# Tile loop of a fused decoder kernel: a tile's outputs and the next tile's transposes in one section behind all projections of a step, the transposes in the gates' banks

## What is computed

```python
gate, hBC, dt = x @ in_proj_w.T, split              # 8192 gate, 8192 + 2*8*128 conv channels, 128 dt
hBC = silu(causal_conv4(hBC) + conv_b)              # 4 taps along the tokens
hs, Bm, Cm = split(hBC)
L = exp(segsum(dt * -exp(A_log)))                   # decay from token to token, per head
y = (Cm @ Bm.T * L) @ (hs * dt) + hs * D            # per head, 128 x 128 tokens
g = y * silu(gate)
g = g * rsqrt(mean over a group's 1024 channels of g*g + eps) * norm_w
x = layernorm(x + g @ out_proj_w.T)
```

## Time and profile before

| | |
|---|---|
| median of the runs shown | 1745.28 us |
| the profiled execution: its own time | 1743.17 us |
| its span, first to last instruction | 1741.5 us |
| TensorE matmul busy | 1659.1 us (95%) |
| VectorE busy | 1196.1 us (69%) |
| ScalarE busy | 1103.3 us (63%) |
| GpSimd busy | 710.6 us (41%) |
| ACT_TABLE_LOADs at L531 / L512 / L546 | 64 / 71 / 8, mean 1283 ns |
| mean granted TensorE clock | 0.988 |

### The profile page before, as it was taken

One profiled execution on the slowest core, in us unless ns is written; L12 is line 12 of the kernel. 1 busy time (PEld: TensorE's weight loads), 2 busy tenths in 40 slices (PEclk: granted clock), 3 DMA queues, 4 the chain that ended last, 5 costly groups with the idle time before them and its releaser, 6 DMA issues.

```text
span 1741.5 us, 26304 instructions
## 1 busy us (share of the span) xinstructions
PE 1659.1 (95%) x9160; PEld 1275.5 (73%) x9160; DVE 1196.1 (69%) x2257; ACT 1103.3 (63%) x2352; POOL 710.6 (41%) x588
## 2 busy tenths in 40 slices
PE   6899999999999999999999999999999987889998
PEld 4777787778777877787778777877787765444656
DVE  4775758675867586758685868586858676896443
ACT  3675668575847594759474948494849482996231
POOL 3363536352626263626361636164616352331000
PEclk8999999999999999999999999999999988999999
DMA  5232213221323131313131313131413273001000
GB/s 200 70 113 73 97 63 120 73 97 55 122 78 98 49 121 64 118 43 128 55 127 43 127 54 128 43 122 48 140 34 115 65 104 111 1 1 37 13 13 24
DMA packets 76551, 138.88 MB, mean 80 GB/s; under 512 B 6786, under 2 KB 13954, under 8 KB 76164
## 3 DMA queue, kind: packets, MB, share of 16 engines
q1 hardware_dynamic: 76420, 137.21, 24.9%
HBM read 134.55 MB, written 2.63 MB: 79 GB/s over the span
## 4 chain that ended last, share of the span: by engine, by line
PE 44%; DVE 33%; ACT 15%; issue 6%; DMA 1%; SPq 1%; POOL 0%; DVEq 0%; ACTq 0%
DVE conv L729 13%; PE ps_hs L1093 6%; PE ps_hs L1095 6%; PE ps_hs L1094 6%; ACT ps_dec L531 6%; DVE xdt L753 4%; DVE m_sb L762 4%; ACT L531 3%; ACT sq_tmp L541 3%; PE ps_hs L246 3%; PE ps_y L1320 3%; PE ps_hs L1282 3%; PE ps_dec L1282 3%; PE ps_hs L248 3%; PE ps_hs L247 3%
## 5 line engine op out<-in xcount | busy, mean ns | idle before, releaser
L378 POOL TENSOR_SCALAR_AFFINE_SELECT cum_bc<-cum_bc 128x1024 f32<-128x1024 f32 x128 | 141.4, 1105 | 501.5 <-DMA cum_bc<-cum_scratch 501.5
L729 DVE SCALAR_TENSOR_TENSOR conv<-ps_hs,cw,conv 128x508 f32<-128x508 f32 (+2 forms) x432 | 319.6, 740 | 36.8 <-ACT conv L495 26.6
L531 ACT ACTIVATE ps_dec<-cum_bc,neg_cum 128x128 f32<-128x128 f32 x1024 | 308.8, 357 | 0.8
L762 DVE TENSOR_TENSOR m_sb<-ps_dec,cb 128x512 f32<-128x512 f32 x256 | 169.6, 686 | 154.6 <-ACT ps_dec L531 154.6
L246 PE MATMUL ps_hs<-x_hi,w_hi 128*128 128x512 f32 x576 | 231.9, 403 | 15.6 <-DVE conv L729 7.6
L246 PE MATMUL ps_gate<-x_hi,w_hi 128*128 128x512 f32 x576 | 239.5, 416 | 0.0
L495 ACT ACTIVATE conv<-ps_hs,cbias,cw 128x512 f32<-128x512 f32 x144 | 110.6, 769 | 189.5 <-PE ps_hs L248 189.5
L248 PE MATMUL ps_gate<-x_hi,w_lo 128*128 128x512 f32 x576 | 226.3, 393 | 0.0
L1093 PE MATMUL ps_hs<-wo_hi,g_hi 128*128 128x512 f32 x512 | 204.4, 399 | 22.8 <-DVE acc L889 8.4
L247 PE MATMUL ps_hs<-x_lo,w_hi 128*128 128x512 f32 x576 | 225.6, 392 | 0.0
L248 PE MATMUL ps_hs<-x_hi,w_lo 128*128 128x512 f32 x576 | 225.6, 392 | 0.0
(11 more groups left out here) (141 smaller groups left out, 3092.8 us busy)
## 6 DMA issues: line engine op xcount, KB each, us to landing
cum_bc<-cum_scratch SPq DMA_DIRECT2D x128, 512.0 KB, 4.0
w_raw<-w_in SPq DMA_DIRECT2D x145, 256.0 KB, 4.6
wo_raw<-w_out SPq DMA_DIRECT2D x64, 256.0 KB, 4.9
g_acc<-x_t SPq DMA_DIRECT2D x4, 512.0 KB, 6.8
acc<-x_nat SPq DMA_DIRECT2D x1, 2048.0 KB, 9.4
k_rep<-ctx_t SPq DMA_DIRECT2D x8, 256.0 KB, 12.6
out<-y_out SPq DMA_DIRECT2D x8, 256.0 KB, 2.0
wg_sb<-w_gate SPq DMA_DIRECT2D x1, 1792.0 KB, 12.4
```

Source lines behind the costliest of these rows:

```text
L531: x = sc.activation(ps_dec[e][:, cols], cum_bc[bh][:, e, cols], ACT.Exp, bias=neg_cum[:, bh * HB + b, head:head + 1])
L729: v.scalar_tensor_tensor(out=dst, in0=src, scalar=cw[:, at, TAPS - 1 - n:TAPS - n], in1=dst, op0=ALU.mult, op1=ALU.add).then_inc(S["tap"], 1)
L762: v.tensor_tensor(flat(m_sb[:, q]), ps_dec[q % 2][:, :], flat(half(cb, q // 2)), ALU.mult)\
```

## The change

Every engine's order in the tile loop is rewritten. TensorE issues heads and gates of step s+1, both halves each, then (each fourth tile) the out-products of the tile before, then outputs(t, 0), outputs(t, 1) and the eight transposes of step s+1, now into ps_gate; they wait for both gates of that tile to have been read (sg_ok), and the next step's gates wait for scale_dt (xdt_ok). Combine, squares and g_low of a tile move into the step behind it on VectorE, ScalarE and GpSimd. ScalarE's order in a tile step becomes: decay 0, squares half 0 of the tile before, first_tap, squares half 1, decay 1, first_tap, silu, decay 2, gate, silu, decay 3, gate, scale_out. The sums of out-products (`keep_products`) stand behind decay 3 on VectorE. outputs(t, 0) also wait for both g_low of the tile before. In a step of B and C the out-products, square_sums and cb_products stand behind the projections. The diff, cut:

```diff
@@ -401,10 +401,14 @@
                 if s + 2 < STEPS:
...
                 if holds_bc(s):
+                    if s:
+                        add_square(tile_at(s - 1), 0)
+                        add_square(tile_at(s - 1), 1)
                     continue
...
                 j = t % TPH
-                if j:
+                if t % TPG:
+                    add_square(t - 1, 0)
                     add_square(t - 1, 1)
@@ -416,9 +420,8 @@
                 pool.wait_ge(S["wo_hi_ok"], t + 1)
...
                                  ALU.subtract).then_inc(S["wo_lo_ok"], 1)
-                add_square(t, 0)
-                if j == TPH - 1:
-                    add_square(t, 1)
+            add_square(TILES - 1, 0)
+            add_square(TILES - 1, 1)
             pool.wait_ge(S["gate_ps"], 2 * STEPS)
@@ -524,6 +527,8 @@
                     act.wait_ge(S["neg_cum_ok"], bh + 1)
...
                     act.wait_ge(S["bc_ok"], 2 * t + bh + 1)
+                if t % TPG == 0 and bh == 0:
+                    act.wait_ge(S["cb_sb"], 2 * (t // TPG) + e + 1)
                 need(act, S["m_ok"], 4 * t + q - 1)
@@ -550,51 +555,61 @@
                     first_tap(0, sub, h)
...
                     silu(0, sub, h)
+            def scale_out(t):
+                act.wait_ge(WO_IN[t % 2], 16 * (t // 2) + 16)
+                need(act, S["wo_lo_ok"], t - 1)
+                sc.activation(wo_sc[:, t % 2, :], wo_raw[:, t % 2, :], ACT.Copy, scale=nw[:, t:t + 1])\
+                    .then_inc(S["wo_sc_ok"], 1)
             for s in range(STEPS):
...
                     if s:
-                        root_group(s // PER - 1)
+                        squares(tile_at(s - 1), 0)
                     first_tap(s + 1, 0, 0)
+                    if s:
+                        squares(tile_at(s - 1), 1)
                     first_tap(s + 1, 0, 1)
...
                 t = tile_at(s)
-                j = t % TPH
+                inner = t % TPG > 0
+                if t and not inner:
+                    root_group(t // TPG - 1)
                 decay(t, 0)
-                decay(t, 1)
-                if j:
-                    squares(t - 1, 1)
+                if inner:
+                    squares(t - 1, 0)
                 if more:
                     first_tap(s + 1, 0, 0)
-                decay(t, 2)
-                decay(t, 3)
+                if inner:
+                    squares(t - 1, 1)
+                decay(t, 1)
                 if more:
...
                     silu(s + 1, 0, 0)
+                decay(t, 2)
+                if more:
                     if holds_bc(s + 1):
...
                         gate(s + 1, 0)
-                act.wait_ge(WO_IN[t % 2], 16 * (t // 2) + 16)
-                need(act, S["wo_lo_ok"], t - 1)
-                sc.activation(wo_sc[:, t % 2, :], wo_raw[:, t % 2, :], ACT.Copy, scale=nw[:, t:t + 1])\
-                    .then_inc(S["wo_sc_ok"], 1)
+                    silu(s + 1, 0, 1)
+                decay(t, 3)
                 if more:
-                    silu(s + 1, 0, 1)
                     if holds_bc(s + 1):
...
                         gate(s + 1, 1)
-                squares(t, 0)
-                if j == TPH - 1:
-                    squares(t, 1)
+                scale_out(t)
                 if more and holds_bc(s + 1):
...
                     silu(s + 1, 1, 1)
+            squares(TILES - 1, 0)
+            squares(TILES - 1, 1)
             root_group(GROUPS - 1)
@@ -752,7 +767,7 @@
                 dve.wait_ge(S["tr_ok"], 2 * t + r + 1)
...
                     half(xdt, r).rearrange("p b (e d) -> p b e d", e=2),
-                    ps_y[r][:, :].rearrange("p (b e d) -> p b e d", b=HB, e=2),
+                    ps_gate[r][:, :].rearrange("p (b e d) -> p b e d", b=HB, e=2),
                     half(dt_tok, r)[:, :, 2 * t:2 * t + 2].unsqueeze(3).broadcast_to([P, HB, 2, HD]),
@@ -790,46 +805,10 @@
             taps(0, 1, 0)
...
             dve.wait_ge(S["x_in"], 16)
-            for s in range(STEPS):
...
+            def keep_products(t):
+                first = t % TPG < TPH
                 g = t // TPG
-                j = t % TPH
...
                 if first and g:
@@ -844,13 +823,64 @@
                         v.tensor_copy(g_acc[:, b, :], ps).then_inc(S["gacc_ok"], 1)
...
                         v.tensor_tensor(g_acc[:, b, :], g_acc[:, b, :], ps, ALU.add).then_inc(S["gacc_ok"], 1)
-                    if holds_bc(s + 1) and b % 2:
-                        if b < 4:
-                            taps(s + 1, 1, b // 2)
-                if not first:
-                    dve.wait_ge(S["ss_ps"], g + 1)
-                    v.tensor_scalar(rstd_g[:, :], ps_y[0][:, 0:BATCH], 1.0 / (TPG * P), EPS, ALU.mult, ALU.add)\
-                        .then_inc(S["rstd_v"], 1)
+            for s in range(STEPS):
+                more = s + 1 < STEPS
+                if holds_bc(s):
+                    g = s // PER
+                    t = tile_at(s - 1)
+                    if s:
+                        combine(t, 0)
+                        combine(t, 1)
+                    taps(s + 1, 0, 0)
+                    if s:
+                        g_low(t, 0)
+                        taps(s + 1, 0, 1)
+                        g_low(t, 1)
+                        keep_products(t)
+                        dve.wait_ge(S["ss_ps"], g)
+                        v.tensor_scalar(rstd_g[:, :], ps_y[0][:, 0:BATCH], 1.0 / (TPG * P), EPS, ALU.mult, ALU.add)\
+                            .then_inc(S["rstd_v"], 1)
+                    keep_cb(g, 0)
+                    keep_cb(g, 1)
+                    if s == 0:
+                        for h in range(2):
+                            dve.wait_ge(S["cum_tr"], h + 1)
+                            v.tensor_scalar(half(neg_cum, h), ps_y[h][:, :].rearrange("p (b h) -> p b h", b=HB),
+                                            -1.0, None, ALU.mult).then_inc(S["neg_cum_ok"], 1)
+                        taps(s + 1, 0, 1)
+                    continue
+                t = tile_at(s)
+                inner = t % TPG > 0
+                if inner:
+                    combine(t - 1, 0)
+                    combine(t - 1, 1)
+                else:
+                    dve.wait_ge(S["cb_sb"], 2 * (t // TPG) + 2)
+                scale_dt(t, 0)
+                scale_dt(t, 1)
+                decay(t, 0)
+                if more:
+                    taps(s + 1, 0, 0)
+                decay(t, 1)
+                if inner:
+                    g_low(t - 1, 0)
+                if more:
+                    taps(s + 1, 0, 1)
+                decay(t, 2)
+                if inner:
+                    g_low(t - 1, 1)
+                decay(t, 3)
+                if more and holds_bc(s + 1):
+                    taps(s + 1, 1, 0)
+                    taps(s + 1, 1, 1)
+                if inner and t % TPH == 0:
+                    keep_products(t - 1)
+            combine(TILES - 1, 0)
+            combine(TILES - 1, 1)
+            g_low(TILES - 1, 0)
+            g_low(TILES - 1, 1)
             def row_stats(stage, b):
@@ -1045,8 +1075,8 @@
                 if holds_bc(s):
                     pe.wait_ge(S["tap"], 3 * (conv_at(s) + 2 + h) + 3)
-                else:
-                    pe.wait_ge(S["sg_ok"], 2 * tile_at(s) + h + 1)
+                elif h == 0:
+                    pe.wait_ge(S["xdt_ok"], 2 * tile_at(s) + 2)
             def cb_products(s):
@@ -1067,19 +1097,22 @@
                         mm = pe.transpose(ps_y[h][:, b * P:(b + 1) * P], src[:, at:at + SEQ], ident[:, :])
                     mm.then_inc(S[done], 1)
-            def transposes(s, r):
+            def transposes(s):
                 t = tile_at(s)
-                pe.wait_ge(S["silu_ok"], conv_at(s) + r + 1)
-                need(pe, S["g_lo_ok"], 2 * t + r - 1)
-                for b in range(HB):
-                    mm = pe.transpose(ps_y[r][:, b * P:(b + 1) * P], hs[s % 2][:, r * HB + b, :], ident[:, :])
-                mm.then_inc(S["tr_ok"], 1)
+                pe.wait_ge(S["silu_ok"], conv_at(s) + 2)
+                pe.wait_ge(S["sg_ok"], 2 * t + 2)
+                for r in range(2):
+                    for b in range(HB):
+                        mm = pe.transpose(ps_gate[r][:, b * P:(b + 1) * P], hs[s % 2][:, r * HB + b, :], ident[:, :])
+                    mm.then_inc(S["tr_ok"], 1)
             def outputs(t, bh):
                 pe.wait_ge(S["m_ok"], 4 * t + 2 * bh + 2)
-                pe.wait_ge(S["xdt_ok"], 2 * t + bh + 1)
+                if bh == 0:
+                    pe.wait_ge(S["xdt_ok"], 2 * t + 2)
+                    need(pe, S["g_lo_ok"], 2 * t)
                 for b in range(HB):
@@ -1114,13 +1147,32 @@
                 heads(0, h)
...
                 gates(0, h)
+            def group_products(t, early):
+                done = BATCH * (t // TPH)
+                pe.wait_ge(S["wo_lo_ok"], t + 1)
+                for b in range(2):
```

(110 more changed lines are left out.)

## The result

The changed kernel takes 2077.16 us (median of 4 runs, 2076.8 to 2077.19) against 1744.48 for the kernel before, measured beside it: ratio 1.191, with an interval of 1.189 to 1.193. The profiled execution spans 2075.5 us at a mean granted clock of 0.929; before it was 1741.5 at 0.988.

A forecast was written before the change was run, and what follows sets the result against it. ScalarE's table loads were to replace TensorE as the bound, with a plain step of 19.03 us: 1743.2 + 250 = 1993, 1995 beside the median, plus 114 for the clock, 2109, say 2108 us; range 1980 to 2165.

The forecast's parts named there:

- loads bind and the clock falls: Favoured case: ScalarE's table loads bind and TensorE's clock falls in most steps; 2108 us, range 2050 to 2165, chance 0.68.
- the sum without the clock: Whole kernel with the clock unchanged: +250 us, 1993 for the profiled execution, 1995 beside the median.
- the clock's term: TensorE's low clock after lulls around the outputs: 1.95 us per step, 14.5 per group, 116 less 2 in all.
- Table loads: ScalarE, tile step: six loads instead of two, 1.39 us each, 5.5 us more; plain step 19.03 us, near 390 loads.
- Nobody else is late: Plain step: VectorE, GpSimd and TensorE deliver in time for ScalarE; VectorE's 12.05 us of work fit.
- one sign of being wrong: Tile loop: a wait on GpSimd's masks, xdt or g_low, held to be early, would show the prediction wrong.
- Steps with out-products: Tile loop: two steps from t%8 = 4 take 57.2 us, the group's end 55.7, the interval behind it 19.3.
- until TensorE has again been busy for some us (22.7): TensorE's low clock starts at 15 to 18.5 in the cycle and lasts to 22.7, nearest to the 6.8 us row.
- Mean under 0.9: Sign to look for: TensorE's granted clock falls in the loop, to a mean under 0.9.
- The rival that the outputs between the two idle parts are activity enough to keep the clock up: TensorE's lull: loads bind but the clock holds; 1995 us, between 1975 and 2015, chance 0.18.
- The gain on TensorE: TensorE, tile step: two seams less and no change from transposes to outputs, 0.3 us per step, 19 us at most.
- The rival "faster": Fewer TensorE seams decide, each added load costing less than 0.13 us: 1725 us, chance 0.04.

The follow-up runs named there:

- the sixth experiment: The changed kernel filled with 13 useless matmuls between outputs half 0 and half 1 of each tile step except t%8 = 4: 2003.31 us, ratio 1.150.
- the third experiment: The kernel before with only ScalarE's order altered, to the changed kernel's alternation of Exp and Silu with six loads per step: 2320.75 us, ratio 1.332.

## Why the prediction was right, and where it was off

It was 2108 with the case "loads bind and the clock falls", whose own range of 2050 to 2165 held the 2077. The error is 31 us: the sum without the clock was 8 too low, the clock's term 40 too high.

**Table loads: right.** The forecast was near 390 loads at 1.39 us; there are 388, and a pair costs 2.82 (1.41 each). ScalarE's step laid out by starts gave 19.03; with the clock held it is 19.06. The Trainium skill, "ScalarE: Activation LUTs", section What ACT_TABLE_LOAD costs, has a drain beside the load, about 2.66 us together. An estimate from that figure makes the step 5.1 us longer, 24.1; the runs show 19.06 and no such drain.

**Nobody else is late: right for the time, though one sign of being wrong did come.** In the tile loop GpSimd and xdt never show among TensorE's waits. The wait on g_lo shows (75.2 us in all, 1.6 each), and the prediction listed such a wait as a sign of being wrong, while its own cycle has g_low ready at 13.6 and outputs half 0 waiting until 13.7. The wait stands inside the idle time that ScalarE leaves, and the 19.07 us step with the same wait of 1.50 shows that it costs nothing at full clock.

**Steps with out-products: right within 0.5 us at full clock.** With the clock held (the sixth experiment), the pair of steps t%8 = 4 and 5 takes 19.06 + 37.92 = 57.0 (57.2 forecast), the group's end 56.2 (55.7), the interval behind it 19.34 (19.3). The whole group is 208.8 against 208.3. Eight times that half microsecond is 4 of the 8 us. The other 4 are nearly the 4.8 us of the three groups whose out-products met a low clock even with the filling (210.4 to 210.6 for the group).

**The clock: right in kind, 1.5 times too dear.** The mechanism shows as described: idle of 1.52 and 3.21 us around the first outputs, a fall, outputs at 1.98 us instead of 1.09, transposes at 1.84 to 1.97 instead of 1.07, and a late first_tap. In the group of tiles 16 to 24 the clock costs 5.2 us in the steps of tiles 17 to 19, 1.4 in the product pair (58.4 against 57.0), 1.2 in the step behind it and 1.9 at the end (58.1 against 56.2). That is 9.8, not 14.5, and 8 x 9.8 = 78 is close to the 79 that were taken away with the lull.

Two terms of the prediction were too large. The first is the count of steps that pay. It charged the first step of a group (1.95) and the products of t%8 = 4 (1.0), and neither pays: tile 16's interval is 19.35, with out-products ahead of it and the clock at 1.00 until 514.7, and the stretch with the products is 37.92 in the changed kernel and in the filled one. These two are 2.95 of the 4.7 us per group. The second is "until TensorE has again been busy for some us (22.7)", the length of the low stretch, taken from the 6.8 us row. A low stretch lasts 3.4 or 6.8 us here, 4.9 on average. Where it lasts 6.8 the price is the forecast one, 1.9 against 1.95 (steps of 20.94 and 21.01); where it lasts 3.4 it ends within the transposes or the first head matmuls, and the price is 1.2 to 1.4 (20.46 and 20.48, with a wait of 1.28 at first_tap in the latter). That is the other 1.8. "Mean under 0.9" was wrong for the same reasons: 0.929.

The rule that was named there, of the Trainium skill, "TensorE: Matmul & The Clock Gate", section HAM oscillation, holds in this trace: in the group of tiles 16 to 24 the clock falls anew in seven of the eight steps. The rival that the outputs between the two idle parts are activity enough to keep the clock up is thus refuted; it took 13 more matmuls to do that.

**The gain on TensorE: too small by half, and hidden.** Priced at 19 us at most, it is 46 with two loads. Per step it was 0.46 and not 0.3: TensorE's own period goes from 14.30 (the transposes at 431.61 and the next at 445.91) to 13.85. The 19.7 us of waits that vanish around the out-products were not in the sum at all. In the changed kernel none of this is seen, since a plain step doesn't wait for TensorE, and its waits for g_acc are 15.0 us as before; so the forecast time didn't suffer.

**The rival "faster"** asked for loads under 0.13 us each, and gave 1725. Its condition can be met by placing instead of by a cheaper load: with the exponentials together it is 1697.

## What to carry to other kernels

Before an engine's work is interleaved with that of another, write down the order in which ScalarE will meet its functions and count the changes of table: here some four more in each of 64 steps turned a gain of 46 us into a loss of 333. Where a second engine becomes the bound by some microseconds per round, look at what the lull does to TensorE's clock as well; it added 74 us to the 306 of the loads. How the idle time is cut up counts too: with six loads in a step, three waits of 2.1, 1.3 and 1.1 us left the clock low for 140 us of the span, and waits of 1.5 and 3.2 us close together for 297. And a change that loses may hold one that wins: the same regrouping, with the exponentials of a step kept together, beats both kernels.

## What the runs showed that was not expected

A wait did not hide a table load here: in the third experiment ScalarE is idle for 3.01 us until VectorE's taps are done, and only behind that comes the load of 1.28 us.

Work without use can pay. 702 idle matmuls in lulls of about 3.3 us took 74 us off a kernel whose bound is another engine; in the one step where TensorE has a full queue they cost their full 3.2 us.

A low stretch can be as short as 3.4 us: 38 of the 61 are. The rows shown before the change had 6.8 and 10.2, though that trace has one of 3.4 too. Which length comes depends on where in the lull the clock falls, as far as two cases show: in tile 17's step it fell at 535.2, early in the lull of 534.75 to 537.96, and stayed low for 6.8 us; in tile 18's it fell at 559.1, just as the outputs behind the lull had begun, and stayed low for 3.4.
